# Value products of two attention parts of a decoder layer issued in larger groups: cross values by two blocks, self values by eight heads

## The reference

```python
x = layernorm(x + self_attn(x))        # 16 heads of 16, causal, 256 x 256 scores
x = layernorm(x + cross_attn(x, ctx))  # 16 heads of 64, 256 x 77 scores
x = layernorm(x + ffn(x))              # 256 -> 1024 -> 1024 -> 256, weights of +1 and -1, relu
```

## Time and profile before

| what | value |
|---|---|
| runs | 2332.79 us median of 3 (2332.78 to 2335.61) |
| profiled execution | 2333.06 us, its span 2331.3 us |
| mean granted clock of PE | 0.987 |
| PE busy | 2233.6 us, 96% of the span |
| DVE busy | 1485.0 us, 64% |
| ACT busy | 970.2 us, 42% |
| POOL busy | 482.0 us, 21% |
| one pass of the loop | 66.13 us |

### The profile page before, as it was taken

The page is one execution under the profiler, slowest core; times in us unless marked ns, Lnnn a source line. Parts: engine busy times, 40 slices in busy tenths (PEclk is TensorE's granted clock), DMA queues, the critical chain, the costliest instruction groups (busy, mean ns, idle before and its releaser), DMA issues.

```text
span 2331.3 us, 52778 instructions
## 1 busy us (share of the span) xinstructions
PE 2233.6 (96%) x18516; PEld 1847.7 (79%) x18516; DVE 1485.0 (64%) x4685; ACT 970.2 (42%) x1797; POOL 482.0 (21%) x751
## 2 busy tenths in 40 slices
PE   7967899999999999999999999999999999999997
PEld 6856787888888888788888888888888888888876
DVE  3435666667667666667676666676676666676763
ACT  3313444444444444444444444444444444444432
POOL 2001212222222122212222222222221222122220
PEclk9978999999999999999999999999999999999999
DMA  6753332132333331233333322323333212233300
GB/s 209 228 115 53 54 58 45 39 50 37 56 56 56 56 50 41 42 44 49 56 56 56 56 42 39 47 41 56 56 56 56 48 40 44 40 53 56 56 25 10
DMA packets 150504, 135.85 MB, mean 58 GB/s; under 512 B 47746, under 2 KB 141986, under 8 KB 150402
## 3 DMA queue, kind: packets, MB, share of 16 engines
q1 hardware_dynamic: 150468, 135.37, 31.3%
HBM read 39.10 MB, written 28.59 MB: 29 GB/s over the span
## 4 chain that ended last, share of the span: by engine, by line
PE 81%; DVE 10%; issue 4%; ACT 3%; DMA 2%; POOL 1%; SPq 0%; DVEq 0%; POOLq 0%
PE ps L1028 10%; PE ps L1029 9%; PE ps L1169 9%; PE ps L988 8%; PE ps L1155 6%; PE ps L1011 5%; PE ps L1141 4%; PE ps L1082 4%; PE ps L1069 4%; PE ps L997 4%; DVE max L736 3%; PE ps L1039 3%; PE ps L1040 2%; PE ps L970 2%; PE ps L977 2%
## 5 line engine op out<-in xcount | busy, mean ns | idle before, releaser
L1028 PE MATMUL ps<-r_h,w 128*128 128x256 f16 x2048 | 464.4, 274 | 1.9 <-DVE r_l L682 1.9
L1029 PE MATMUL ps<-r_l,w 128*128 128x256 f16 x2048 | 462.1, 273 | 0.0
L471 ACT ACTIVATE r_h<-ps 128x512 f16<-128x512 f32 x256 | 152.6, 596 | 524.1 <-PE ps L1029 516.4
L697 DVE CUSTOM_DVE_ANT_0 junk<-ps,causal 128x128 bf16<-128x128 f32 (+1 forms) x1024 | 316.2, 353 | 60.1 <-PE ps L1058 53.8
L419 POOL TENSOR_TENSOR p<-p,inv 128x308 f32<-128x308 f32 x256 | 179.0, 699 | 479.5 <-DVE inv L753 479.5
L682 DVE SCALAR_TENSOR_TENSOR r_l<-ps,r_h 128x512 f16<-128x512 f32 x256 | 176.1, 688 | 119.5 <-ACT r_h L471 119.5
L524 ACT ACTIVATE probs<-ps 128x768 f32<-128x768 f32 x256 | 206.9, 809 | 106.9 <-PE ps L1069 106.8
L412 POOL TENSOR_SCALAR_AFFINE_SELECT probs<-probs 128x512 f32<-128x512 f32 x256 | 163.3, 638 | 393.8 <-ACT probs L524 393.7
L1028 PEld LDWEIGHTS ps<-r_h,w 128*128 128x128 f16 x2048 | 200.1, 98 | 49.6 <-issue 23.5
L1029 PEld LDWEIGHTS ps<-r_l,w 128*128 128x128 f16 x2048 | 200.9, 98 | 20.7
L758 DVE TENSOR_TENSOR o_l<-ps,o_h 128x512 fp32r<-128x512 f32 x128 | 88.5, 691 | 191.0 <-ACT o_h L516 190.6
(11 more groups left out here) (140 smaller groups left out, 4729.3 us busy)
## 6 DMA issues: line engine op xcount, KB each, us to landing
q_st<-o_h SPq DMA_DIRECT2D x192, 128.0 KB
k_bd<-o_h SPq DMA_DIRECT2D x192, 128.0 KB, 6.7
q<-q SPq DMA_DIRECT2D x128, 128.0 KB, 2.1
v_scratch<-v_out SPq DMA_DIRECT2D x44, 224.0 KB, 2.3
k_bd<-k_scratch SPq DMA_DIRECT2D x64, 154.0 KB
v<-v_scratch SPq DMA_DIRECT2D x32, 308.0 KB
x_in<-in_x SPq DMA_DIRECT2D x32, 256.0 KB, 4.6
out<-y SPq DMA_DIRECT2D x32, 256.0 KB, 2.2
```

What stands on the lines that cost most here:

```text
L697: dve.tensor_tensor_reduce(out=junk[:, e, b * P:b * P + width], in0=ps[:, bank + b, e * width:(e + 1) * width], in1=causal[:, (1 - b) * P: ...
L1028: pe.matmul(dst, w1[:, kk, m * P:(m + 1) * P], r0_h[:, kk, :], start=kk == 0, stop=False)
L1029: last = pe.matmul(dst, w1[:, kk, m * P:(m + 1) * P], r0_l[:, kk, :], start=False, stop=kk == KF - 1)
```

## The change

PE's order of the value products is changed, with what has to follow from it:

- `cross_values(i, u)` now takes two blocks, 2u and 2u+1, at once, and waits for `cross_probs` of both. On PE it stands where `cross_transposes(2u+2)` has been issued, in place of one block at a time. `cross_transposes(i, 3)` is put ahead of `scores_by_query(i + 1, 1)`. On ACT the four `cross_output` move to other places in the order.
- `values(i, m)` now takes eight heads (four pairs) and waits for POOL's mask of the fourth. There are two calls a pass instead of four. For that there are six buffers of probabilities: four in `probs` (which had the room of six times 512 floats, and has the same size now) and two in `p2`, which is free in that part of the pass. `scores_by_key` 6 and 7 and the feed-forward work (`filler0`) close ranks around them.
- ACT: `self_probs(i, 7)` ahead of the first relu. DVE: `transposed_x(i + 1)` (xt_l, L705) ahead of `self_output(i, 0)`.

The diff:

```diff
@@ -114,9 +114,7 @@
         xt_l = sb("xt_l", [P, KD, S], F32R)
         o2_h = sb("o2_h", [P, KX, S], F32R)
         o2_l = sb("o2_l", [P, KX, S], F32R)
-        probs = sb("probs", [P, 6, 512], F32)
-        probs_flat = probs[:].rearrange("p a b -> p (a b)")
-        pr = probs_flat[:, 0:4 * 768].rearrange("p (n a b) -> p n a b", n=4, a=2)
+        probs = sb("probs", [P, 4, 2, 3 * P], F32)
         qk_h = o2_h[:, 0:2 * KD, :]
         qk_l = o2_h[:, 2 * KD:4 * KD, :]
         o_h = sb("o_h", [P, KD, S], F32R)
@@ -128,6 +126,12 @@
         o_c = q2[:, 4:6, :]
         s_c = q2[:, 6:8, :]
         p2 = sb("p2", [P, KX, 4, SK], F32)
+        probs_more = p2[:].rearrange("p a b c -> p (a b c)")[:, 0:2 * 6 * P].rearrange("p (n a b) -> p n a b", n=2, a=2)
+
+        def pr(n):
+
+            return probs[:, n % 6] if n % 6 < 4 else probs_more[:, n % 6 - 4]
+
         p2_t = sb("p2_t", [SK, 4, 512], F32)
         x2 = sb("x2", [P, TB, D], F32)
         x2t_h = sb("x2t_h", [P, KD, S], F16)
@@ -408,7 +412,7 @@
                 for n in range(NP):
                     pool.wait_ge(a_p, nth(i, NP, n + 1))
                     pool.sem_inc(passed_pool, 1)
-                    diag = pr[:, n % 4, :, 0:2 * P].rearrange("p a (b q) -> p a b q", b=2)
+                    diag = pr(n)[:, :, 0:2 * P].rearrange("p a (b q) -> p a b q", b=2)
                     pool.affine_select(out=diag, in_=diag, compare_op=ALU.is_ge, fill=0.0, base=0,
                                        pattern=[[0, 2], [0, 2], [1, P]], channel_multiplier=-1).then_inc(g_p, 1)
                 if g is not None:
@@ -518,14 +522,14 @@
             def self_probs(i, n):
 
                 act.wait_ge(pe_st, nth(i, NP, n + 1))
-                if n >= 4:
-                    act.wait_ge(pe_pv, nth(i, 4, n // 2 - 1))
+                if n >= 6:
+                    act.wait_ge(pe_pv, nth(i, 2, 1))
                 b = 4 + 2 * (n % 2)
-                act.activation(pr[:, n % 4, :, :], ps[:, b:b + 2, P:512], ACT.Exp, scale=SELF_SCALE).then_inc(a_p, 1)
+                act.activation(pr(n), ps[:, b:b + 2, P:512], ACT.Exp, scale=SELF_SCALE).then_inc(a_p, 1)
 
             def self_output(i, m):
 
-                act.wait_ge(pe_pv, nth(i, 4, 2 * m + 2))
+                act.wait_ge(pe_pv, nth(i, 2, m + 1))
                 act.activation(o_raw[:, 2 * m:2 * m + 2, :], ps[:, 2 + m, :], ACT.Copy).then_inc(a_o, 1)
 
             def self_output_high(i, m):
@@ -543,9 +547,9 @@
                 self_probs(i, 5)
                 self_output(i, 0)
                 self_probs(i, 6)
+                self_probs(i, 7)
                 if not first:
                     relu(0, r0_h, pe_z0, a_r0, f, 0)
-                self_probs(i, 7)
                 if more:
                     transposed_x(i + 1)
                 self_output(i, 1)
@@ -583,14 +587,14 @@
                 cross_exp(i, 6)
                 cross_probs(i, 2)
                 cross_exp(i, 7)
+                cross_output(i, 0)
                 cross_probs(i, 3)
-                cross_output(i, 0)
                 cross_probs(i, 4)
+                cross_output(i, 1)
                 cross_probs(i, 5)
-                cross_output(i, 1)
                 cross_probs(i, 6)
+                cross_output(i, 2)
                 cross_probs(i, 7)
-                cross_output(i, 2)
                 cross_output(i, 3)
                 if not first:
                     residual(f, first_f)
@@ -769,9 +773,9 @@
                     layer_norm_stats(2, y3, g)
                 if not first:
                     relu_low(0, r0_h, r0_l, a_r0, d_r0, f, 0)
+                if more:
+                    transposed_x(i + 1)
                 self_output(i, 0)
-                if more:
-                    transposed_x(i + 1)
                 if not first:
                     relu_low(1, r0_h, r0_l, a_r0, d_r0, f, 1)
                 self_output_low(i, 0)
@@ -1070,17 +1074,18 @@
                                          k_bd[:, n, e, kb * P:(kb + 1) * P], q_st[:, n, :], start=True, stop=True)
                 last.then_inc(pe_st, 1)
 
-            def values(i, g):
-
-                pe.wait_ge(g_p, nth(i, NP, 2 * g + 2))
-                if g == 0:
+            def values(i, m):
+
+                pe.wait_ge(g_p, nth(i, NP, 4 * m + 4))
+                if m == 0:
                     pe.wait_ge(a_nm, nth(i, 2, 2))
-                c = (g % 2) * S
-                for b in range(TB):
-                    for j in range(4):
-                        src = pr[:, (2 * g + j // 2) % 4, j % 2, (1 - b) * P:(3 - 2 * b) * P]
-                        last = pe.matmul(ps[32 * j:32 * j + 32, 2 + g // 2, c + b * P:c + S], v[:, b, 4 * g + j, :], src,
-                                         start=b == 0, stop=b == 1)
+                for g in (2 * m, 2 * m + 1):
+                    c = (g % 2) * S
+                    for b in range(TB):
+                        for j in range(4):
+                            src = pr(2 * g + j // 2)[:, j % 2, (1 - b) * P:(3 - 2 * b) * P]
+                            last = pe.matmul(ps[32 * j:32 * j + 32, 2 + m, c + b * P:c + S], v[:, b, 4 * g + j, :], src,
+                                             start=b == 0, stop=b == 1)
                 last.then_inc(pe_pv, 1)
 
             def transposed_inputs(j):
@@ -1142,20 +1147,20 @@
                                             p2[:, t, 2 * b + e, :], ident[:])
                 last.then_inc(pe_p2t, 1)
 
-            def cross_values(i, t):
-
-                u = t // 2
-                pe.wait_ge(a_p2t, nth(i, KX, t + 1))
-                if t % 2 == 0 and u < 2:
+            def cross_values(i, u):
+
+                pe.wait_ge(a_p2t, nth(i, KX, 2 * u + 2))
+                if u < 2:
                     pe.wait_ge(a_q2, nth(i, 4, u + 3))
-                elif t % 2 == 0:
+                else:
                     pe.wait_ge(a_o2h, nth(i, 4, u - 1))
                     pe.wait_ge(d_o2l, nth(i, 4, u - 1))
-                for e in range(2):
-                    last = pe.matmul(ps[64 * e:64 * e + 64, 6 + u % 2, (t % 2) * S:(t % 2 + 1) * S],
-                                     v2[:, (2 * t + e) * XD:(2 * t + e + 1) * XD], p2_t[:, t % 4, e * S:(e + 1) * S],
-                                     start=True, stop=True)
-                last.then_inc(pe_o2, 1)
+                for t in (2 * u, 2 * u + 1):
+                    for e in range(2):
+                        last = pe.matmul(ps[64 * e:64 * e + 64, 6 + u % 2, (t % 2) * S:(t % 2 + 1) * S],
+                                         v2[:, (2 * t + e) * XD:(2 * t + e + 1) * XD], p2_t[:, t % 4, e * S:(e + 1) * S],
+                                         start=True, stop=True)
+                    last.then_inc(pe_o2, 1)
 
             def cross_projection(i, t):
 
@@ -1199,21 +1204,19 @@
                 scores_by_key(i, 2)
                 filler2(1)
                 scores_by_key(i, 3)
-                values(i, 0)
                 filler2(2)
                 scores_by_key(i, 4)
                 if f is not None:
                     if g is not None:
                         pe.wait_ge(d_y3, nth(g, 2, 1))
                     transposed_x2(f)
+                values(i, 0)
                 scores_by_key(i, 5)
                 filler2(3)
-                values(i, 1)
+                scores_by_key(i, 6)
                 filler0(0)
-                scores_by_key(i, 6)
+                scores_by_key(i, 7)
                 filler0(1)
-                scores_by_key(i, 7)
-                values(i, 2)
                 if more:
                     pe.wait_ge(a_p, nth(i, NP, NP - 1))
                     transposed_inputs(i + 1)
@@ -1221,7 +1224,7 @@
                     pe.wait_ge(d_y3, nth(g, 2, 2))
                 filler0(2)
                 filler0(3)
-                values(i, 3)
+                values(i, 1)
 
                 filler0(4)
                 filler0(5)
@@ -1271,24 +1274,20 @@
                 cross_transposes(i, 2)
                 cross_values(i, 0)
                 cross_scores(i, 7)
+                cross_transposes(i, 3)
                 if more:
                     scores_by_query(i + 1, 1)
-                cross_transposes(i, 3)
+                cross_transposes(i, 4)
                 cross_values(i, 1)
-                cross_transposes(i, 4)
-                cross_values(i, 2)
                 cross_transposes(i, 5)
-                cross_values(i, 3)
                 cross_projection(i, 0)
                 cross_transposes(i, 6)
-                cross_values(i, 4)
+                cross_values(i, 2)
                 cross_projection(i, 1)
                 cross_transposes(i, 7)
-                cross_values(i, 5)
                 cross_projection(i, 2)
-                cross_values(i, 6)
                 cross_projection(i, 3)
-                cross_values(i, 7)
+                cross_values(i, 3)
                 cross_projection(i, 4)
                 cross_projection(i, 5)
```

(2 more changed lines are left out.)

## The result

| | before | after |
|---|---|---|
| median of 19 runs | 2335.02 us (2332.3 to 2341.46) | 2339.93 us (2336.57 to 2343.39) |
| ratio | | 1.0018, 95% interval 1.0011 to 1.0025 |
| span of the profiled execution | 2331.3 us | 2339.9 us |
| PE busy | 2233.6 us (96%) | 2178.9 us (93%) |
| one pass of the loop | 66.13 us | 66.26 us |

The kernel became slower by 0.18%: little, but the interval does not hold 1. PE lost 55 us of busy time and the kernel lost 5 us of time: a saving and a cost of almost the same size.

The account below looks back on a forecast made before the run. PE, busy 96% of the span, was taken to bound the kernel. Cross +0.91 and self -0.44 gave +0.47 us a pass, x 31 = +14.6 on the profiled 2333.06; less 0.3 for the median, 2347.3 us, range 2329 to 2357.

Parts of the forecast that it names:

- middle step: One block's cross value products inside a group on PE, neither entering nor leaving narrow tiles: 0.22 us, called least sure.
- wait ahead of the first pair: PE, after cross_transposes(2), must now wait for ACT's cross_probs(1): 0.72 us a pass.
- wait ahead of the second pair: PE waits for cross_probs(3), behind block 7's scores, subtraction, exponential and cross_output(0): 1.47 us a pass.
- saved by grouping cross values: Fewer entries into and exits from narrow tiles on PE, fewer slowed successors: 1.28 us a pass saved.
- self part: Value calls of eight heads save 0.40, freed queries 0.20, new waits cost 0.16: -0.44 us a pass.
- From such an end to PE it is 0.15: Time from the end of an awaited record on another engine to PE's start: 0.15 us.
- two waits of 0.07 and 0.09 for POOL: Both self value calls on PE wait for POOL's mask of their last pair; called a near tie.
- The 0.20 that I booked for the freed queries: With xt_l moved ahead of DVE's reciprocal, the next sequence's queries on PE no longer wait: 0.20 us a pass saved.
- savings and waits cancel: Rival: middle step of 0.18 and waits shorter by a tenth, about +0.05 us a pass, 2329 to 2337; chance 0.2.
- my own case: The forecast case: cross +0.91 and self -0.44 us a pass, 2338 to 2354 us; chance 0.52.
- The waits are hidden: Rival: only the switches count, 1.88 us a pass saved, 2275 us; chance of faster in all 0.14.
- The near tie at layer0 block 6: Second relu_low on DVE ends about 1057.5, PE needs it at 1057.6: no cost, no room.

Follow-up runs that it names:

- e7_dve_only: The kernel before with only DVE's transposed_x(i + 1) moved ahead of self_output(i, 0); 2332.4 us, ratio 0.9987 to the kernel before.
- e6_self_old_dve: Self part of the change alone, with DVE's transposed_x left behind self_output(i, 0) as before; 2345.5 us, ratio 1.0038 to the kernel before.
- e3_scores_first: The changed kernel with PE's cross_scores(i, 7) put ahead of the first pair of cross values; 2295.2 us, ratio 0.9829 to the kernel before.
- e4_probs_first: The changed kernel with ACT's cross_probs(i, 3) put ahead of cross_output(i, 0); 2323.6 us, ratio 0.9946 to the kernel before.
- e5_both: The changed kernel with the edits of e3_scores_first and e4_probs_first together; 2283.3 us, ratio 0.9773 to the kernel before.
- e9_split_last: e8_exp_last with the last pair of cross values split into single blocks around cross_projection(i, 3); 2293.8 us, ratio 0.9825 to the kernel before.
- e8_exp_last: e5_both with ACT's cross_exp(i, 7) moved behind cross_probs(i, 3); 2282.5 us, ratio 0.9772 to the kernel before.

## Why the prediction was wrong

The forecast was +14.6 us, to 2347.3; measured +4.9, to 2339.93. Direction and mechanism were right, and so were both places of waiting; the size was off by a factor of 3, because +0.47 us a pass was a small difference of large terms, and each term was off by up to a fifth, all to the same side. Neither of the two signs of being wrong that I had named came (a second wait under 0.7 us, a much cheaper middle step), so they did not guard against this error.

| term, us a pass | forecast | measured |
|---|---|---|
| wait ahead of the first pair | 0.72 | 0.63 (1020.83 to 1022.02 is 1.19; transposes with entry took 0.56) |
| wait ahead of the second pair | 1.47 | 1.38 (1026.37 less 1024.46 less 0.53) |
| saved by grouping cross values | 1.28 | 1.34 (the two waits less 0.67) |
| self part | -0.44 | -0.53 |
| sum | +0.47 | +0.14 (the pass: +0.13) |

- **The step that failed: "From such an end to PE it is 0.15".** I read the time from the end of another engine's record to the start of the waiting PE record off one place, and put it into all four waits. At the two pairs it is 0.05 and 0.06: `cross_probs(1)` ends at 1021.97 and PE starts at 1022.02; `cross_probs(3)` ends at 1026.31, PE at 1026.37. This is 0.2 of the 0.34 us. In the very same pass the place I had read it from shows 0.15 again, so the row was not an accident, but neither was it a price for other places. The kernel before holds a wait of the short kind as well, of full-width f16 products for DVE, first on PE, then on DVE, in the same pass:

```profile
1042.94 0.28 PE L1039 MATMUL ps<-w,r_h 128*128 128x256 f16 x1 [0.24 <-DVE r_l L682]
```

```profile
1042.19 0.69 DVE L682 SCALAR_TENSOR_TENSOR r_l<-ps,r_h 128x512 f16<-128x512 f32 x1 [0.40 <-ACT r_h L471]
```

DVE ends at 1042.88 and PE starts 0.06 later. With both ends carried, 0.05 and 0.15, the sum would have been +0.1 to +0.5.
- **Self part.** The two waits of 0.07 and 0.09 for POOL came as 0.05 (1051.90 to 1052.48 is 0.58, not 0.53) and 0.01 at most. This is another 0.1 of the 0.34, most of it again the 0.15, at the second call. At the first PE starts 0.13 after the mask's end (1051.71 + 0.64 = 1052.35), so there the price was nearly right. At the second it is 0.05 in most passes, as here, first POOL, then PE:

```profile
1124.23 0.64 POOL L416 TENSOR_SCALAR_AFFINE_SELECT probs<-probs 128x512 f32<-128x512 f32 x1 [0.29 <-ACT probs L528]
```

```profile
1124.60 0.38 PE L1015 MATMUL ps<-x2t_l,w 128*128 128x256 f16 x2
1124.92 0.86 PE L1087 MATMUL ps<-p,v 128*32 128x256 f32 x16
```

The rest of the saving came out as worked. The 0.20 that I booked for the freed queries was the right price in the wrong account: alone it is worth nothing (`e7_dve_only`), and with the grouping its absence costs 0.93 (`e6_self_old_dve`). The move is what makes later first outputs affordable.
- **Cross saving.** 0.06 above the forecast. The middle step, which I called the least sure, is right: a pair takes 1.01 to 1.02. The price of one switch, summed from five rows as 0.33, is 0.36 measured by itself.
- **The chain.** DVE behind `cross_scores(7)`, the exponential, `cross_output(0)`, `cross_probs(3)`: each link shows (`e3_scores_first` breaks the first, `e4_probs_first` takes out `cross_output(0)`). From the start of `cross_scores(7)` to the second pair it is 3.34 us, forecast 3.41.
- **The rivals.** By its size, +0.13 a pass, the result is next to "savings and waits cancel" (about +0.05); as a time, 2339.93 lies in the low end of my own case (2338 to 2354), which is partly luck, since the kernel before itself came to 2335.02 in 19 runs instead of 2332.79 in three. Half of that rival's mechanism came, the waits were shorter (by 0.02 to 0.09 us each); the cheaper middle step did not. Its sum was also wrong as written: eight middle steps at 0.18 take off 0.32, and a tenth of the waits' 2.35 is 0.24, which from +0.47 gives about -0.1, not +0.05. "The waits are hidden" did not happen in this kernel, but its gain was there to be had: 1.66 of 1.88 us a pass in `e5_both`. The near tie at layer0 block 6 did not turn into a wait with the whole change, where the reciprocal ahead of `relu_low` starts 1.42 us before the queries; it did in `e7_dve_only`, where that is 1.11 us.
- The rule of the Trainium skill ("TensorEngine Tiling", section Tiling Modes: changing the mode drains the engine) agrees with the longer steps at entry and exit in these traces; `e9_split_last` gives one way in and out its price here, 0.36 us. That the engine drains in them no run shows.

## What to carry to other kernels

Grouping narrow-tile products saves a fixed price for each switch, but the group's start is set by its last operand and everything queued behind it on PE starts later: follow the longest thing behind it round through the other engines, and move that ahead of the group first. Here one such move was worth 1.34 us a pass, some 42 us, where the whole change cost 5. Where a forecast is a small difference between a saving and a wait, take each latency in it from several rows and carry both ends; and when a mended wait gives no time, look for the next operand that comes last, as `e8_exp_last` did.

## What the runs showed of the hardware

- Going into 64-wide column tiles and out again, between full-width fp32r products, costs PE 0.36 us in all (`e9_split_last`), a little more than half of it behind the last narrow product: an exit of 0.09 us, and a first full-width product that is slowed by 0.10 us. For 32-wide tiles with f16 products behind them, where the slowing is 0.01, no run has the price by itself; from the self part, 0.53 saved less 0.20 for the queries plus 0.06 of new waits over two switches, I estimate 0.2 us each.
- From the end of another engine's record to the start of the PE record that waited for it, PE idle in between, there are two values, each the same to 0.002 us in every pass of the loop. 0.15 us: full-width fp32 transposes (1016.46 to 1016.61 before), full-width fp32r scores that waited for DVE (1015.49 to 1015.64 before), and the queries in `e6_self_old_dve`. 0.05 to 0.06 us: the narrow cross values, and full-width f16 products (1042.88 to 1042.94 before; 1054.81 to 1054.87 in `e7_dve_only`). So the width of the tile alone does not decide it, nor does the engine waited for: DVE stands in both groups. What does was not tested and stays open.
